# A decoder layer with eight routed experts: scattering expert tiles with an add into one cleared row per token instead of storing two rows per token

## What is computed

```
gate_scores = softmax(x @ Wg.T)
topk_val, topk_idx = top_k(gate_scores, 2)
topk_val = topk_val / (topk_val.sum(-1) + 1e-9)
comb = (one_hot(topk_idx, 8) * topk_val[..., None]).sum(-2)
for e in range(8):
    h = x @ W1[e].T + b1[e]
    a, b = split(h, 2)                 # 512 columns each
    g = a * sigmoid(b)
    out += (g @ Wo.T + bo) * comb[..., e:e+1]
x = layernorm(x + out)
```

## Time and profile before

| | us |
|---|---|
| median of 3 runs | 1431.65 |
| lowest and highest of the 3 | 1428.14, 1438.48 |
| the profiled execution, whole | 1429.97 |
| its span, first to last instruction | 1428.1 |
| busy in the span: PE, DVE, ACT, POOL | 1272.3, 1136.6, 742.4, 635.3 |

### The profile page before, as it was taken

How to read it: one execution, slowest core, us unless ns; L and a number is a source line. 1 busy time by engine, 2 the same in 40 slices (tenths; PEclk the granted TensorE clock), 3 DMA queues, 4 the chain that set the end, 5 groups by cost and what they waited for, 6 DMA issues and landing times. The chain is left out here.

```text
span 1428.1 us, 29996 instructions
## 1 busy us (share of the span) xinstructions
PE 1272.3 (89%) x7734; PEld 898.8 (63%) x7735; DVE 1136.6 (80%) x3121; ACT 742.4 (52%) x1716; POOL 635.3 (44%) x978
## 2 busy tenths in 40 slices
PE   6888899999899999999998559999999999968886
PEld 4443555556555555555553347888888888858786
DVE  0356788888888888888887778888888888859998
ACT  1225677777777777777777512222223332214444
POOL 3001244544454445445435343333333333348886
PEclk9999999999999999999999669999999999989999
DMA  7435475565674765665742854433343433379995
GB/s 165 99 74 87 84 120 116 117 128 124 121 132 114 131 120 119 129 125 112 132 96 77 332 181 135 133 128 131 132 134 134 134 129 129 133 270 330 334 341 186
DMA packets 171744, 212.39 MB, mean 149 GB/s; under 512 B 20032, under 2 KB 142912, under 8 KB 167424
## 3 DMA queue, kind: packets, MB, share of 16 engines
q1 hardware_dynamic: 147792, 144.32, 43.2%
q0 software_dynamic: 17488, 55.02, 10.3%
q10 hardware_dynamic: 6368, 11.89, 2.4%
HBM read 125.76 MB, written 85.71 MB: 148 GB/s over the span
## 5 line engine op out<-in xcount | busy, mean ns | idle before, releaser
L981 DVE TENSOR_REDUCE negmax<-psS 128x2 f32<-128x512 f32 x512 | 349.2, 686 | 99.6 <-PE psS L677 82.5
L820 ACT ACTIVATE probs<-psT 128x512 f32<-128x512 f32 x512 | 303.3, 598 | 168.8 <-PE psT L687 160.4
L1425 ACT ACTIVATE sig<-hb 128x512 f32<-128x512 f32 x135 | 85.4, 632 | 287.2 <-DVE hb L1501 280.1
L677 PE MATMUL psS<-kstack,qstack 96*128 96x256 bf16 x1024 | 195.0, 272 | 36.0 <-DVE kstack L1079 12.7
L687 PE MATMUL psT<-qstack,kstack 99*128 99x512 bf16 x512 | 193.7, 380 | 4.6 <-ACT probs L820 4.5
L1307 POOL DMA_INDIRECT g_rows<-g,slot x135 | 134.7, 998 | 70.0 <-issue 66.5
L677 PEld LDWEIGHTS psS<-kstack,qstack 96*128 96x128 bf16 x1024 | 92.3, 104 | 93.1 <-DVE negmax L981 34.6
L430 POOL DMA_INDIRECT lists<-x,slots x128 | 130.9, 1022 | 33.1 <-issue 30.2
L570 PE MATMUL psO<-probs,vaug 128*32 128x512 f32 x1024 | 137.2, 608 | 0.4 <-ACT probs L820 0.4
L1512 DVE SCALAR_TENSOR_TENSOR g<-g,xe,sig 128x512 f32<-128x512 f32 x135 | 101.4, 751 | 26.3 <-DVE g L1508 17.0
L1344 PE MATMUL psHb<-w_hi,xet_hi 128*128 x270 | 117.8, 436 | 0.0
(11 more groups left out here) (207 smaller groups left out, 2929.2 us busy)
## 6 DMA issues: line engine op xcount, KB each, us to landing
rows<-g_rows SPq DMA_DIRECT2D x32, 1024.0 KB, 8.1
qstack<-q_parts SPq DMA_DIRECT2D x192, 128.0 KB
xe<-lists SPq DMA_DIRECT2D x135, 133.0 KB, 2.1
q_parts<-qpart SPq DMA_DIRECT2D x32, 384.0 KB
sums<-x SPq DMA_DIRECT2D x32, 264.0 KB
x2in<-sums SPq DMA_DIRECT2D x32, 264.0 KB, 4.7
xt<-in_x_t SPq DMA_DIRECT2D x32, 256.0 KB
xres<-in_x SPq DMA_DIRECT2D x32, 256.0 KB
```

What stands on the lines that cost most here:

```text
L677: last = mm(psS[:, u % 2, hh * S:(hh + 1) * S], qstack[0:KROWS, b1.s4, 2 * hp + hh, c * P:(c + 1) * P], kstack[0:KROWS, b1.s4, :], start=T ...
L820: nc.scalar.activation(probs[:, u % PT, :], psT[:, u % 2, :], ACT.Exp, scale=SELF_SCALE).then_inc(sm["exp_done"], 1)
L981: v.tensor_reduce(negmax[:, b1.s2, 2 * hp:2 * hp + 2, c], psS[:, u % 2, :].rearrange("p (h k) -> p h k", h=2), AX.X, ALU.max, negate=True) ...
```

## The change

`g_rows` gets one row per token (10240 rows with the pads instead of 20480). It has to be zero before the first scatter: POOL clears an SBUF tile `zeros` at the start, and SP writes it to `g_rows` by 20 DMAs of 1 MB, one at the end of each of the steps 2 to 21 of the attention stage. The scatter of a tile becomes one with `compute_op=add`: the DMA adds the tile's row to what stands there. Two scatters that hit the same token must not be in flight together. A token is at most once in each expert's list, so tiles of one expert may overlap; the first tile of an expert waits until the three scatters before it have landed. Inside the loop that is decided by a table, `turn_tab`, which POOL reads for every tile into a register; for the first six tiles and the last two, which are written out, every scatter waits for the ones before it. `away` falls away; the token's number is copied to `place` by POOL and to `slot` by DVE, as before in time. `lists` loses a column. In the last stage SP loads 512 KB a pair, `row_sum` is gone, and PE transposes `rows` itself.

```
-    ROW = D + E + 2
+    ROW = D + E + 1
...
+        def clear_rows(t):
+            places = dram["g_rows"].rearrange("(p k) h -> p k h", p=P)
+            n = t.n - 2
+            if 0 <= n < places.shape[1] // ZROWS:
+                sp.wait_ge(dram["zeros_made"], 1)
+                sp.dma_start(places[:, n * ZROWS:(n + 1) * ZROWS, :],
+                             zeros[:, :].unsqueeze(1).to_broadcast([P, ZROWS, zeros.shape[1]])
+                             ).then_inc(dram["rows_cleared"], 16)
...
                                  ).then_inc(sm[f"q_stacked{b.s2}"], 16)
+            clear_rows(t)
...
+            pool.memset(zeros[:, :], 0.0).then_inc(dram["zeros_made"], 1)
             pool.memset(pad[:, :, :], 0.0).then_inc(sm["pool_chain"], 1)
...
             if e == 4:
+                act.wait_ge(dram["rows_cleared"], 16 * (dram["g_rows"].shape[0] // (P * ZROWS)))
                 act.wait_ge(dram["pads_stored"], 32)
...
-                v.tensor_copy(x2[:, b6.s2, :, D + E + 1], topf[:, b6.s2, :, 0]).then_inc(sm["comb_ready"], 1)
+                last.then_inc(sm["comb_ready"], 1)
...
         def step(t):
             o = t.back(2)
+            turn = None
+            for m in range(1, 4):
+                before = o.back(m)
+                if active(o) and (not o.fixed or 8 <= o.n < TILES - 2):
+                    turn = pool.value_load(turn_tab[0:1, bass.ds(o.n, 1)], min_val=0, max_val=16) if turn is None else turn
+                    wait(pool, f"g_stored{before.s4}", ring(before) + turn)
+                elif active(o) and before.n >= 0:
+                    wait(pool, f"g_stored{before.s4}", ring(before) + 16)
+            if active(o):
+                wait(pool, "g_ready", done(o))
             if active(t):
                 wait(pool, f"xe_loaded{t.s4}", ring(t) + 16)
-                wait(pool, "g_ready", done(o))
-                pool.tensor_tensor(away[:, t.s4:t.s4 + 1], xe[:, t.s4, FIRST:FIRST + 1],
-                                   expf[:, bass.ds(t.n, 1)], ALU.subtract).then_inc(sm["away_ready"], 1)
+                pool.tensor_tensor(place[:, t.s4:t.s4 + 1], xe[:, t.s4, ID:ID + 1], zero[:, :], ALU.add
+                                   ).then_inc(sm["place_ready"], 1)
             if active(o):
                 pool.indirect_dma_start(out=dram["g_rows"], out_offset=bass.IndirectOffsetOnAxis(
-                    ap=slot[:, o.s4:o.s4 + 1], axis=0), in_=g[:, o.s4], in_offset=None
+                    ap=slot[:, o.s4:o.s4 + 1], axis=0), in_=g[:, o.s4], in_offset=None, compute_op=ALU.add
                     ).then_inc(sm[f"g_stored{o.s4}"], 16)
+        pool.wait_ge(dram["rows_cleared"], 16 * (dram["g_rows"].shape[0] // (P * 4)))
+        pool.wait_ge(sm["turns_ready"], 1)
+        pool.memset(zero[:, :], 0.0).then_inc(sm["zero_ready"], 1)
+        pool.wait_ge(sm["zero_ready"], 1)
...
         def pair_step(t):
-            if active(t, PAIRS):
-                wait(pool, f"rows_loaded{t.s4}", ring(t) + 16)
-                for c in range(QC):
-                    wait(pool, "g_transposed", QC * t.n + c - 3)
-                    pool.tensor_tensor(row_sum[:, t.s2 * QC + c], rows[:, t.s4, c, 0:H], rows[:, t.s4, c, H:2 * H], ALU.add
-                                       ).then_inc(sm["rows_added"], 1)
...
                     for k in range(HC):
                         last = nc.tensor.transpose(psG[:, c, k * P:(k + 1) * P],
-                                                   row_sum[:, t.s2 * QC + c, k * P:(k + 1) * P], ident[:, :])
+                                                   rows[:, t.s4, c, k * P:(k + 1) * P], ident[:, :])
...
+        link(v.tensor_tensor(turn[:, 1:TILES], expf[:, 1:TILES], expf[:, 0:TILES - 1], ALU.not_equal))
+        v.tensor_scalar(turn_tab[:, 1:TILES], turn[:, 1:TILES], 16.0, None, ALU.mult).then_inc(sm["turns_ready"], 1)
...
-                v.scalar_tensor_tensor(slot[:, i.s4:i.s4 + 1], away[:, i.s4:i.s4 + 1], 0.0, xe[:, i.s4, ID:ID + 1],
-                                       ALU.not_equal, ALU.add)
+                v.tensor_copy(slot[:, i.s4:i.s4 + 1], place[:, i.s4:i.s4 + 1])
```

More of the change, by code:

```diff
@@ L123, in attention @@
     rden = sb("rden", [P, 2, QC * 8])
-    with nc.sbuf_tensor("pad", [P, 2 * E, ROW], F32) as pad:
+    ZROWS = 4
+    with nc.sbuf_tensor("pad", [P, 2 * E, ROW], F32) as pad, nc.sbuf_tensor("zeros", [P, dram["g_rows"].shape[1]], F32) as zeros:
         pass
@@ L1105, in step @@
                 for c in range(QC):
-                    v.scalar_tensor_tensor(x2[:, b6.s2, c, D:D + E], gexp[:, b6.s2, c, :],
+                    last = v.scalar_tensor_tensor(x2[:, b6.s2, c, D:D + E], gexp[:, b6.s2, c, :],
                                                   gden[:, b6.s2, c:c + 1], hotsum[:, b6.s2, c, :], ALU.mult, ALU.mult)
-                v.tensor_copy(x2[:, b6.s2, :, D + E + 1], topf[:, b6.s2, :, 0]).then_inc(sm["comb_ready"], 1)
+                last.then_inc(sm["comb_ready"], 1)
                 if not b6.fixed or b6.n >= 2:
-                    v.tensor_scalar(x2[:, b6.s2, :, D + E], x2[:, b6.s2, :, D + E], float(4 * S), None, ALU.add)
+                    v.tensor_scalar(x2[:, b6.s2, :, D + E], x2[:, b6.s2, :, D + E], float(2 * S), None, ALU.add)
                 wait(dve, "counted", done(b6))
@@ L1147, in experts @@
     I32 = mybir.dt.int32
-    rows, row_sum, x2in, y, result = (dram[k] for k in ("rows", "row_sum", "x2in", "y", "result"))
+    rows, x2in, y, result = (dram[k] for k in ("rows", "x2in", "y", "result"))
     w1_hi, w1_lo, b1, bo = dram["w1_hi"], dram["w1_lo"], dram["b1"], dram["bo"]
@@ L1170, in experts @@
     exp_tab = sb("exp_tab", [P, TILES], I32)
+    turn = sb("turn", [P, TILES])
+    turn_tab = sb("turn_tab", [P, TILES], I32)
     pad_tab = sb("pad_tab", [P, E], I32)
@@ L1177, in experts @@
     xet_lo = sb("xet_lo", [P, 2, DC * P], F32R)
-    away = sb("away", [P, 4])
+    place = sb("place2", [P, 4])
+    zero = sb("zero", [P, 1])
     slot = sb("slot", [P, 4], U32)
@@ L1276, in load_rows @@
         def load_rows(t):
-            wait(sp, "rows_added", done(t.back(4), QC))
+            wait(sp, "g_transposed", done(t.back(4), QC))
             sp.dma_start(rows[:, t.s4], stored_rows[bass.ds(t.n, 1)].rearrange("o p c h -> (o p) c h")
@@ L1396, in pair_step @@
                 if active(t, PAIRS):
-                    wait(pe, "rows_added", QC * t.n + c + 1)
+                    if c == 0:
+                        wait(pe, f"rows_loaded{t.s4}", ring(t) + 16)
                     wait(pe, "gt_split", QC * t.n + c - 1)
@@ L1502, in step @@
                                 ).then_inc(sm["hb_ready"], 1)
-                wait(dve, "away_ready", done(i))
+                wait(dve, "place_ready", done(i))
                 wait(dve, f"g_stored{i.s4}", ring(i))
-                v.scalar_tensor_tensor(slot[:, i.s4:i.s4 + 1], away[:, i.s4:i.s4 + 1], 0.0, xe[:, i.s4, ID:ID + 1],
-                                       ALU.not_equal, ALU.add)
+                v.tensor_copy(slot[:, i.s4:i.s4 + 1], place[:, i.s4:i.s4 + 1])
                 wait(dve, "a_product", done(i))
@@ L1573, in decoder_layer @@
             "sum": nc.dram_tensor("sums", (T, D + E), F32, kind="Internal").ap(),
-            "g_rows": nc.dram_tensor("g_rows", (2 * (T + 2 * E * P), H2 // 2), F32, kind="Internal").ap(),
-            "lists": nc.dram_tensor("lists", (E * (stride + P), D + E + 2), F32, kind="Internal").ap(),
-            "pad_rows": nc.dram_tensor("pad_rows", (E * P, D + E + 2), F32, kind="Internal").ap(),
+            "g_rows": nc.dram_tensor("g_rows", (T + 2 * E * P, H2 // 2), F32, kind="Internal").ap(),
+            "lists": nc.dram_tensor("lists", (E * (stride + P), D + E + 1), F32, kind="Internal").ap(),
+            "pad_rows": nc.dram_tensor("pad_rows", (E * P, D + E + 1), F32, kind="Internal").ap(),
             "stride": stride,
@@ L1586, in decoder_layer @@
             dram[name] = ctx.enter_context(nc.sbuf_tensor(name, shape, F32))
-        for name in ("biases_loaded", "w1_rounded", "w1_split", "wo_loaded", "wo_rounded", "wo_split", "pads_stored"):
+        for name in ("biases_loaded", "w1_rounded", "w1_split", "wo_loaded", "wo_rounded", "wo_split", "pads_stored", "zeros_made", "rows_cleared"):
             dram[name] = ctx.enter_context(nc.semaphore(name))
@@ L1601, in decoder_layer @@
                 dram["w1_raw"] = w1_raw
-            with (nc.sbuf_tensor("rows", [P, 4, QC, 2 * H], F32) as rows, nc.sbuf_tensor("row_sum", [P, 4, H], F32) as row_sum,
+            with (nc.sbuf_tensor("rows", [P, 4, QC, H], F32) as rows,
                   nc.sbuf_tensor("x2in", [P, 4, QC, D + E], F32) as x2in, nc.sbuf_tensor("y", [P, 4, QC, D], F32) as y):
-                dram.update(rows=rows, row_sum=row_sum, x2in=x2in, y=y)
+                dram.update(rows=rows, x2in=x2in, y=y)
             place("w1_lo", [P, W1], F32R)
```

16 lines of the change are left out of this document (7 added, 9 removed).

## The result

The changed kernel takes 1461.52 us (median of 4 runs, 1454.09 to 1465.81) against 1429.89 for the kernel before: ratio 1.0206, 95% interval 1.0169 to 1.0244. The change makes it slower by 2%; the forecast was 1415 us.

A forecast was written before the change was run, and what follows sets the result against it. PE was taken to bound the expert tiles, DVE, held by POOL's `row_sum`, the last stage. Terms -26.0 + 3.8 + 1.7 + 4.0 + 0.4 (tables) = -16.1 gave 1415 us, range 1400 to 1440.

The forecast's parts named there:

- The other tiles: 0: Expert tiles after the first six scatters: `place` and `slot` stay in time, POOL keeps 0.6 us of slack, no cost.
- L: Time from issue to landing of a scatter with an add, taken as 4.2 us, between 2.9 and 5.0.
- The price of the add: Expert tiles' scatter: 2.9 us plain, plus 0.67 for doubled engine time and 0.6 waiting for the read, 4.2 us.
- The first six scatters, +3.8: Start of the expert tiles: each scatter waits for the one before, `xet_lo` comes late, PE stands still 3.8 us.
- The end of the stage, +1.7: End of expert stage: last scatters land late, SP's loads go 4.2 us later, less 2.6 from shorter work: +1.7 us.
- Clearing, +4: Attention stage: 20 clears of 1 MB ahead of `xt` make it 0.2 us late on average, +4 us.
- Last stage, -26.0: Last stage: without `row_sum` DVE is freed, PE bounds, pairs go from 4.67 to 3.74 us, 28 times: -26.0 us.
- Rival 1: Expert stage: the scatter with the add lands much later, at L = 9 the kernel takes 1461 us; 10%.
- Rival 2: Attention stage: clear goes slower or holds `qstack` too; at 4.0 us it costs 32 instead of 4, 1443 us; 9%.
- Rivals 3 and 4: POOL becomes the tiles' bound, 1459 us, 7%; last stage isn't freed, something else at 4.3 us, 1430 us, 12%.

The follow-up runs named there:

- the run with own rows and the add: Kernel before, each token keeping its two rows, with only the scatter's add and clearing by DMAs of 2 MB: 1523.8 us.
- the early load: Changed kernel with POOL copying weights and row number out of `xe`, so SP loads the tile four on without waiting for `g`: 1428.79 us, ratio 0.9972.
- the combined kernel: Changed kernel with the early load, the table of turns also from the sixth tile and for the last two, clearing behind `xt`: 1410.62 us, ratio 0.9849.

## Why the prediction was wrong

**The other tiles: 0.** This is the step that failed, in the sentence "So nothing is late up to L = 6". It followed `place` and `slot` and found them in time, which they are. It left out the load of the tile four on, which SP issues behind `g`. In the kernel before that load is issued 3.2 us ahead of its transposes and lands 2.1 us after issue: 1.1 us of slack. The add cuts into this from both ends: in the run with own rows and the add SP issues the load 1.32 us after `g`'s end on average instead of 0.89, and the load, which shares the engines with scatters of 32.5 us instead of 10.7, lands after 2.42 us instead of 2.09, the slowest after 3.50. That alone costs 7 us; with scatters held back and let go together it is 26, and where many of them also go out sooner behind `g`, as in the changed kernel (0.62 us instead of 1.26 for the multiples of four), 39. The prediction's words that the engines "don't become the bound" at a share of 0.62 named the wrong test: the share came to 0.76, still under 1, and a load with 1.1 us in hand was late all the same.

**The price of the add.** L was taken as 4.2 us and bounded at 5.0; the waits show 5.0 to 5.2 up to the next `place`. The bytes were mis-sized: a doubling of 0.67 us on each engine was assumed, 30.9 / 16 = 1.9 us came, and the 0.6 us taken for the wait for the read stood on no row. By the packets of the first scatter the bytes begin 2.2 us after issue (1.6 before), take 2.45 us (0.9), and the semaphore counts 0.3 us later (0.35): 5.0 where the plain scatter has 2.9, as was read from its rows. The Trainium skill (Collectives: The Full Stack, "Why ReduceScatter is half of AllGather") puts the price of an add in a reduce-scatter in its two source reads, which halve the rate. Here it was more, 2.9 times the engine time of the plain scatter, and 5.0 us where that rule gave 3.6. POOL's instruction went from 1.00 to 1.56 us, which the prediction held only as a rival at 2.0; as POOL had 1.36 us to spare it never became the bound.

**The first six scatters, +3.8.** The mechanism is there (cycles of 5.0 to 5.8 us on POOL against 4.98 worked out) but the excess grew by 13.2 - 2.6 = 10.6. The prediction let PE wait for `xet_lo` alone; PE waited for `xe`, whose load stands behind the late `g` (waits of 860:900 in the changed kernel):

```profile
PE psX L1391 <- DMA xe<-lists: 7.5, 4, 3.3
```

With the early load, where `xet_lo` is what PE waits for, it is still 10.9 - 2.6 = 8.3, near the 7.8 given for L = 5.0.

**The end of the stage, +1.7.** 6.3; at L = 5.0 the prediction's formula gives 4.1. From the scatter at 1302.36 to the loads at 1318.48 are 16.1 us for three that wait one for another.

**Clearing, +4.** The place and the mechanism were right (`xt` late, nothing else), the size was short: 5.6 with the tables in the profiled execution, 8 to 14 in others. The Trainium skill (DMA: Bandwidth & Descriptors, "Queues, rings and completion order") has descriptors consumed in ring order on each DMA engine. The runs agree: a clear of 2 MB makes `xt` late by up to 4.7 us, and a clear of 1 MB behind `xt` costs 0 to 5 us in all.

**Last stage, -26.0.** -26.4, for the reason given; the run without `row_sum` shows the reason alone. The Trainium skill (SBUF — State Buffer, "Who interferes with whom") has a VectorE instruction with two SBUF inputs contend with a GpSimd instruction that reads SBUF; the rows agree, 2.03 us for two beside `row_sum`, 0.87 without it.

**The rivals.** Rival 1 named 1461 us, which was measured, but by L = 9 and POOL's order; L is about 5, and the wait is PE's for a load. Rival 2's late `xt` came, at 8 to 14 us instead of 32. Rivals 3 and 4 fell: POOL still waits for `g` (its instruction is 1.56 us, not 2.0), and the last stage is freed. No rival had the load of `xe`.

What stays open: why SP's issue behind `g` takes 0.4 us longer beside add scatters, how the loss divides between this and the slower landing, and 1.6 of the 5.3 us that the first tiles of the combined kernel lose beyond those of before (for 3.7 PE waits for `xet_lo` there).

## What to carry to other kernels

When an edit makes a DMA heavier, list the other transfers of that stretch with their slack from issue to use, and ask of each what it loses, even if the engines' share stays under 1. A wait that holds some transfers back also decides when they go out together, so its price and that of the transfer can't be added. A load that stands behind a late result should be freed from it (here by copying nine words out of the buffer) before its neighbours grow.

## What was not expected of the hardware

The add turned 64 packets of 4 KB into 128 of 2 KB per scatter, with 2.9 times the engine time, and lengthened POOL's own instruction from 1.00 to 1.56 us. Three idle instructions ahead of each scatter made the kernel 14 us faster. And in the run without `row_sum` PE kept 3.8 us a pair in the last stage while the profile gave the DMA engines a share of 1.02 at 414 GB/s.
